# An LSTM step on one core: the two seed copies of ScalarE moved directly behind the gates of their halves

## The reference

```
xz = einsum('ntd,dk->ntk', x, Wx) + b          # for all time steps
def step((prev_h, prev_c), xz_t):
    z = xz_t + prev_h @ Wh
    ai, af, ao, ag = split(z, 4, axis=1)
    i, f, o, g = sigmoid(ai), sigmoid(af), sigmoid(ao), tanh(ag)
    next_c = f * prev_c + i * g
    next_h = o * tanh(next_c)
x = x + hs                                      # then: x + adapter(x, cond)
```

## Time and profile before

| what | value |
|---|---|
| time, median of 3 runs | 621.93 us (621.92 to 622.44) |
| span of the profiled execution, first to last instruction | 618.6 us |
| granted TensorE clock, mean | 0.997 of full speed |
| PE / PEld busy | 600.8 us (97%) / 444.2 us (72%) |
| DVE busy | 471.6 us (76%) |
| ACT busy | 386.8 us (63%) |
| POOL busy | 38.6 us (6%) |

### The profile page before, as it was taken

How to read it: one execution, slowest core, us unless ns; L and a number is a source line. 1 busy time by engine, 2 the same in 40 slices (tenths; PEclk the granted TensorE clock), 3 DMA queues, 4 the chain that set the end, 5 groups by cost and what they waited for, 6 DMA issues and landing times.

```text
span 618.6 us, 33951 instructions
## 1 busy us (share of the span) xinstructions
PE 600.8 (97%) x14120; PEld 444.2 (72%) x14120; DVE 471.6 (76%) x2543; ACT 386.8 (63%) x2158; POOL 38.6 (6%) x77
## 2 busy tenths in 40 slices
PE   8689998999999999999999999999999999999997
PEld 5565556777777777777777777777777777777886
DVE  3576667778888888788888888888878888888772
ACT  2365656666666666666666666666666666666662
POOL 3000000000000000000000000000000000000000
PEclk9899999999999999999999999999999999999999
DMA  5993630232333123333321232332122323211201
GB/s 162 233 217 141 181 45 13 38 46 55 55 55 53 32 33 49 54 55 54 56 34 32 47 54 55 54 55 41 38 33 55 55 55 55 44 37 24 54 21 36
DMA packets 31499, 38.74 MB, mean 63 GB/s; under 512 B 3632, under 2 KB 29536, under 8 KB 30321
## 3 DMA queue, kind: packets, MB, share of 16 engines
q1 hardware_dynamic: 31282, 36.51, 30.5%
q0 software_dynamic: 64, 0.07, 0.1%
HBM read 15.59 MB, written 4.19 MB: 32 GB/s over the span
## 4 chain that ended last, share of the span: by engine, by line
PE 95%; DVE 1%; issue 1%; DMA 1%; SPq 0%; ACT 0%; ACTq 0%
PE z L698 36%; PE x_bank L496 18%; PE z_o L698 9%; PE aux L522 8%; PE out_bank L545 7%; PE out_bank L627 3%; PE aux L507 3%; PE aux L474 2%; PE out_bank L577 2%; PE aux L529 2%; PE out_bank L566 1%; PE x_bank L566 1%; DMA seed<-proj 1%; PE x_bank L522 1%; DMA x_nat<-in_x 0%
## 5 line engine op out<-in xcount | busy, mean ns | idle before, releaser
L698 PEld LDWEIGHTS z<-wh,h_t 128*16 128x16 f32 x8160 | 159.8, 96 | 116.8 <-DVE h_t L855 87.1
L698 PE MATMUL z<-wh,h_t 128*16 128x96 f32 x8160 | 233.5, 248 | 4.9 <-issue 2.1
L835 DVE STREAM_TRANSPOSE z<-z 128x96 f32<-128x96 f32 x512 | 151.4, 298 | 86.7 <-PE z L698 67.9
L413 ACT ACTIVATE gates<-z 128x48 f32<-128x48 f32 x512 | 107.7, 210 | 156.9 <-DVE z L835 129.3
L496 PE MATMUL x_bank<-wx,x_t 128*128 128x256 f32 x512 | 156.0, 392 | 0.5 <-ACT x_t L331 0.5
L337 ACT ACTIVATE z<-seed 128x96 f32<-128x96 f32 x512 | 123.7, 242 | 5.8 <-DMA seed<-proj 5.8
L698 PE MATMUL z_o<-wh,h_t 128*16 128x64 f32 x4080 | 106.1, 219 | 0.8 <-issue 0.8
L845 DVE SCALAR_TENSOR_TENSOR prod<-gates 128x32 f32<-128x32 f32 x512 | 97.7, 191 | 0.6
L850 DVE SCALAR_TENSOR_TENSOR gates<-prod 128x16 f32<-128x16 f32 x512 | 84.2, 165 | 8.7
L496 PEld LDWEIGHTS x_bank<-wx,x_t 128*128 128x128 f32 x512 | 80.6, 195 | 6.4 <-issue 1.5
L698 PEld LDWEIGHTS z_o<-wh,h_t 128*16 128x16 f32 x4080 | 81.2, 97 | 1.4 <-issue 1.3
(11 more groups left out here) (114 smaller groups left out, 439.0 us busy)
## 6 DMA issues: line engine op xcount, KB each, us to landing
seed<-proj SPq DMA_DIRECT2D x128, 128.0 KB
w<-in_L_cond_W SPq DMA_DIRECT2D x4, 2048.0 KB, 10.2
x_nat<-in_x SPq DMA_DIRECT2D x32, 128.0 KB, 4.2
out<-y_nat SPq DMA_DIRECT2D x32, 128.0 KB, 4.2
wx<-in_L_cond_Wx SPq DMA_DIRECT2D x2, 512.0 KB, 5.9
wh<-in_L_cond_Wh SPq DMA_DIRECT2D x2, 256.0 KB, 7.1
wh<-in_L_cond_Wh SPq DMA_DIRECT2D x1, 512.0 KB, 6.5
w<-in_L_cond_W SPq DMA_DIRECT2D x1, 256.0 KB, 4.5
```

Source lines behind the costliest of these rows:

```text
L413: act.activation(gates[s % 2][m][:, 0:3 * B].rearrange("p (g b) -> p g b", b=B), zt[m].rearrange("p (g c) -> p g c", c=C)[:, :, 0:B], ACT. ...
L698: ins = pe.matmul(dst, h_prev[:, kc, :], rhs, start=False, stop=(kc == 1), skip_group_check=True)
L835: dve.transpose(zt[m], z_bank[m][:, 0:GC]).then_inc(turned[m], 1)
```

## The change

The seed copy of a half now stands directly behind the tanh of that half's gates, in front of the tanh of o. Its wait for `gates_ready` is gone, since it follows the tanh that raises it. The wait for `seed_loaded` moves from the end of step 6 to the start of step 7.

```diff
+                    if s == TB - 1 and more:
+                        act.wait_ge(seed_loaded[ahead.par], (ahead.turn + 1) * (16 * NQ))
                     gates_of(0)
+                    if more:
+                        seed_bank(ahead.par, s_next, 0)
                     gates_of(1)
+                    if more:
+                        seed_bank(ahead.par, s_next, 1)
                     tanh_o()
                     tanh_cell(0)
-                    if more:
-                        act.wait_ge(gates_ready[0], n)
-                        seed_bank(ahead.par, s_next, 0)
                     tanh_cell(1)
                     if more:
-                        act.wait_ge(gates_ready[1], n)
-                        seed_bank(ahead.par, s_next, 1)
                         act.wait_ge(ht_ready[1], n + 1)
                         seed_o(ahead.par, s_next)
 
-                    if s == TB - 2 and (front or k.p == 0):
-                        ahead = k.plus(1)
-                        act.wait_ge(seed_loaded[ahead.par], (ahead.turn + 1) * (16 * NQ))
```

## The result

The changed kernel takes 618.0 us (median of 4 runs, 616.9 to 618.71), the kernel before in the same comparison 622.18 (621.92 to 623.29). The profiled execution of after took 618.71 us with a span of 616.9. Each run lies 1.8 us above its span, so the profiled execution of before, whose span was 618.6, took about 620.4 and was 1.5 us quicker than its timed runs. Spans of single executions therefore show only part of the difference.

A forecast was written before the change was run, and what follows sets the result against it. The prediction took the kernel as bound by a latency loop between hidden states, closing over half 1. Removing 1.9 us and adding 1.1 gave -0.8, so 621.93 became 621.1 us; forecast's own range 620.5 to 621.8, overall range 619.4 to 623.4.

The forecast's parts named there:

- What the change removes: ScalarE's tanh of cell 1, freed of the seed copy, starts 0.009 us earlier in 216 steps: -1.9 us.
- What it moves: Half 0's copy between ScalarE's two gate tanh: pair taken as 0.28 us, hidden within 0.33, cost 0.
- What it adds: Second wait on step 7's first tanh costs 0.06 us, net +0.04 in each of 25 blocks: +1.1 us.
- the 0.02 that I had coming back in this step: Step 7: tanh of cell 1 gains 0.03 us, 0.02 more than in other steps, offsetting part of the 0.06.
- the sum: Terms -1.9 and +1.1 give -0.8 us on the profiled execution, forecasting 621.1 us.
- the second group waits for half 1 in any case: TensorE's second group needs half 1, ending at 306.74, when the first has had 0.20 us; argued against TensorE gaining.
- TensorE gains too: Rival: TensorE's first group, freed of half 0's copy, starts some 0.04 us earlier: -9.6, 611 us; chance 0.05.
- The base: Timed runs taken to lie 3.3 us above the profiled span, untouched by the change; forecast started from 621.93 us.

The follow-up runs named there:

- the wait alone: The kernel before with only the `seed_loaded` wait moved to the start of step 7, both seed copies left in place: 623.54 us, ratio 1.0034.
- the late stop: Changed kernel, seed wait back at the end of step 6, TensorE's first matmul also waiting for the previous step's cell of half 1: 618.97 us, ratio 0.9963.
- the early and the late run: Changed kernel, seed wait back in step 6, extra TensorE wait: early for prod of half 0, 616.01 us; late for cell of half 1, 618.97 us.

## Why the prediction was wrong

The forecast was -0.8 us and the measurement is 622.18 to 618.0, -4.2. Point by point:

- **What the change removes, -1.9 us: the step that failed in size.** The tanh of cell 1 does start when its cell is there, and ScalarE idles in front of it, as foretold. But recorded alone it lasts 187 ns, where it lasted 180 directly behind another instruction, and so it ends where it did. Ordinary steps kept 2.212 us. Only the first step of a block gained, from 2.279 to 2.270, some 0.3 us in all. (Over all 192 steps the rows of before give 0.043 and 0.035, where the prediction has 0.041 and 0.032.)
- **What it moves, 0: right.** The pair takes 0.28 us, by the rows at 300.07 that I went by. Step 0, where 0.26 was all the room, got no longer.
- **What it adds, +1.1 us: right.** The medians say 2.212 to 2.260, 0.048 in 26 blocks, +1.25 us. (The prediction's 25 blocks at 0.04 make 1.0, not 1.1.) Of the 0.02 that I had coming back in this step, about half came: with the wait alone the step takes 2.27, with the copies moved too 2.26.
- **Missing from the sum: some -4.5 us; the step that failed in kind.** The sum put what the earlier copy of half 0 does for TensorE at nothing, on the ground that the second group waits for half 1 in any case. That holds for the ordinary step. I worked out that step and multiplied. The trace of before also held 22 long steps in blocks 4 to 29, with 4.1 us above their medians, which I never summed. In the two profiled executions that excess fell by 3.3 us and that of blocks 0 to 3 by 1.2. The rival "TensorE gains too" stood at the right wait, the seed copy of half 0, but with the wrong mechanism: it priced the start of the first group at 0.04 in all 240 steps and came to 611 us. That start moved by 0.02 and earned nothing, and the real effect is rare and large.
- **The base.** "The runs lie 3.3 us above the span" mixed two things: 1.8 us around the span, and a profiled execution that was 1.5 us quicker than the median.

The four sizes, -0.3 + 1.25 - 3.3 - 1.2 = -3.6, stand against 583.6 - 580.4 = 3.2 us less from the first `h_t` to the last in the two profiles. What lies around that is 35.0 us in the profile of before and 36.5 in that of after, so the two spans differ by only 1.7.

Shown: the gain is in half 0's copy alone; a late stop of TensorE brings most of the long steps back. Not settled: why blocks 0 to 3 kept their gain of about 1 us with the late stop; how much of a late fetch is the stop and how much the seed and `x` transfers in front of it, which fill the transfer engines until 129.3 us in the case above (q1's packets have a share of 113.1% from 126 to 129.3 us and of 3.1% from there to 131); and why the places are 193 and 194. Rows show when the sequencer gets past its wait and when the packets come; that the stop holds up the fetch is inferred from the two going together in these runs.

## What to carry to other kernels

Before a step's gain is multiplied by its count, sum how far the long steps stand above the median, and look at what they wait for: here "issue" in front of a few loads was worth more than the rearrangement of the ordinary step. Let a semaphore that an engine waits for ahead of its data come early, or try to drop it where another wait covers it: here the early copy of half 0 was worth 5.2 us (616.57 against 621.79), and dropping the wait on top showed no further gain. Put a second wait on an instruction that idles anyway (on the path it cost 0.06 us here), and look which of two waits gets the row of its own (below).

## What the runs showed of the hardware

- TensorE's instruction packets came to 256 instructions each (28,689 beside 112 packets of 16 KB; 28,434 beside 111 without the waits for the seeds). At the places 193 and 194 modulo 256 TensorE stood for 0.19 to 0.58 us eight times in before, from 100 us on, and once, while the kernel starts up, for 1.49 us. That it stood for a late packet is inferred: in seven of the eight the loads went on 1.27 to 1.48 us behind a packet's end.
- A second wait on one instruction cost 0.06 us on ScalarE (0.03 to 0.09 behind the transpose) and on VectorE (step 0, 2.27 to 2.21 without it), though what it waited for had long been there (for at least 4.4 us at the 31 rows of ScalarE in after, for at least 17.3 us at the 30 of VectorE in before). On TensorE one more wait, early met, cost nothing that these runs can tell (616.01 against 615.87 us). The rows show a difference: on ScalarE the wait for the transpose, which ends last, got an `EVENT_SEMAPHORE` of its own (L412, 31 of them in after against 5 in before); it starts 0.03 us behind the transpose, and the tanh 0.06 behind it. On TensorE the wait that ends last, for `h_t`, is on the step's first load itself, and the added one went into the row that the wait for the seeds already had (L688 of the early and the late run, 51 ns, where it has two waits). In both the wait that is written first in the code is the one on the instruction. Whether writing the transpose's wait first would save the 0.06 was not tried.
- The tanh of cell 1 is recorded with 180 ns in before, directly behind another instruction, and with 187 ns in after, by itself (means of 256), so that an earlier start was no earlier end.
